# Scan of a Mamba-2 block: the sums of squares over a row's channels, as eight fp32 products on TensorE in place of a VectorE sum and one product

## What is computed

```python
xBC = silu(causal_depthwise_conv(...)); xb, Bc, Cc = split(xBC)      # before the scan
Y_diag = einsum('bcqhn,bcshn,bhcqs,bcshp->bcqhp', Cm, Bm, Lm, xdt)    # within a chunk of 128 rows
states = einsum('bcqhn,bhcq,bcqhp->bchpn', Bm, decay_states, xdt)     # carried from chunk to chunk
Y_off  = einsum('bcqhn,cbhpn,bhcq->bcqhp', Cm, prevs, exp(dAc))
y = (Y_diag + Y_off).reshape(b, l, h, p) + Dp * x_h
y = y.reshape(b, l, 1024)
y = y * silu(z)
y = y * rsqrt(mean(y * y, axis=-1) + eps) * norm_w                    # the sums of squares of the change
h = residual + y @ out_proj_w                                         # then a second norm, h2
```

## Time and profile before

| what | value |
|---|---|
| median of 3 runs | 1661.74 us (1661.3 to 1663.65) |
| the profiled execution | 1666.47 us |
| its span, first to last instruction | 1664.8 us |
| mean granted TensorE clock | 0.942 |
| TensorE busy | 1445.6 us (87%) |
| VectorE busy | 780.0 us (47%) |
| ScalarE busy | 446.8 us (27%) |
| GpSimd busy | 441.1 us (26%) |
| the scan | about 338 to 646 us |
| one chunk of the scan, in its steady part | 17.50 us |

### The profile page before, as it was taken

The page is one execution under the profiler, slowest core; times in us unless marked ns, Lnnn a source line. Parts: engine busy times, 40 slices in busy tenths (PEclk is TensorE's granted clock), DMA queues, the critical chain, the costliest instruction groups (busy, mean ns, idle before and its releaser), DMA issues. The chain is left out here.

```text
span 1664.8 us, 20088 instructions
## 1 busy us (share of the span) xinstructions
PE 1445.6 (87%) x6651; PEld 1045.3 (63%) x6652; DVE 780.0 (47%) x1357; ACT 446.8 (27%) x924; POOL 441.1 (26%) x486
## 2 busy tenths in 40 slices
PE   5688979769999994999999999999760599999996
PEld 4566768536666663888888888888620355555553
DVE  4857676658998992323232323233544122122121
ACT  4333434345555552212112121121120111111110
POOL 2411111126776764101011111010006222222222
PEclk9899999979999997999999999999985799999998
DMA  8112202352332314801000010000197222223220
GB/s 179 51 51 102 101 28 100 127 171 89 107 116 96 121 58 170 289 17 32 20 25 25 16 34 17 22 0 0 53 364 262 87 78 86 87 82 86 89 77 21
DMA packets 92867, 147.12 MB, mean 88 GB/s; under 512 B 29182, under 2 KB 45566, under 8 KB 92800
## 3 DMA queue, kind: packets, MB, share of 16 engines
q1 hardware_dynamic: 79424, 119.92, 22.0%
q0 software_dynamic: 8800, 25.21, 4.5%
q10 hardware_dynamic: 4576, 1.13, 0.3%
HBM read 91.63 MB, written 58.27 MB: 90 GB/s over the span
## 5 line engine op out<-in xcount | busy, mean ns | idle before, releaser
L1356 PE MATMUL ff_bank<-ff_hT_hi,ff_w_hi 128*128 128x512 f32 x512 | 202.3, 395 | 13.3 <-POOL ff_w_lo L1262 13.3
L1356 PE MATMUL ff_bank<-ff_hT_hi,ff_w_lo 128*128 128x512 f32 x512 | 204.9, 400 | 0.0
L1356 PE MATMUL ff_bank<-ff_hT_lo,ff_w_hi 128*128 128x512 f32 x512 | 203.0, 396 | 0.0
L1797 PE MATMUL ex_bank<-w_gu,xT 128*128 x624 | 193.5, 464 | 1.4 <-ACT xT L1728 0.8
L1322 DVE TENSOR_TENSOR ff_prod<-ff_prod,ff_bank 128x512 f32<-128x512 f32 x64 | 44.0, 688 | 274.7 <-PE ff_bank L1356 266.3
L1262 POOL TENSOR_TENSOR ff_w_lo<-ff_stage,ff_w_hi 128x1024 fp32r<-128x1024 f32 x24 | 57.3, 2393 | 417.2 <-ACT ff_w_hi L1309 413.6
L1797 PEld LDWEIGHTS ex_bank<-w_gu,xT 128*128 128x128 f32 x624 | 116.7, 192 | 60.9 <-issue 3.8
L1767 DVE SCALAR_TENSOR_TENSOR result_rows<-ex_bank,xs,result_rows 128x512 f32<-128x512 f32 x39 | 29.3, 751 | 256.2 <-DMA result_rows<-out_dram,xs 253.6
L479 DVE SCALAR_TENSOR_TENSOR conv_acc<-raw,conv_w,conv_acc 128x512 f32<-128x512 f32 x144 | 114.9, 799 | 62.4 <-ACT raw L296 52.5
L572 PE MATMUL pj_bank<-hT_hi,w_in_hi 128*128 128x512 f32 x336 | 140.3, 418 | 1.6 <-DVE hT_lo L412 1.6
L572 PE MATMUL pj_bank<-hT_lo,w_in_hi 128*128 128x512 f32 x336 | 137.5, 409 | 0.0
(11 more groups left out here) (238 smaller groups left out, 2429.9 us busy)
## 6 DMA issues: line engine op xcount, KB each, us to landing
cv_rows<-cst SPq DMA_DIRECT2D x12, 1024.0 KB, 4.3
cv<-cv_rows SPq DMA_DIRECT2D x16, 768.0 KB, 4.3
sorted_rows<-blank SPq DMA_DIRECT2D x1, 10023.0 KB, 46.0
xs<-sorted_rows SPq DMA_DIRECT2D x39, 257.0 KB, 2.7
zs_rows<-zst SPq DMA_DIRECT2D x8, 1024.0 KB, 6.5
zs<-zs_rows SPq DMA_DIRECT2D x16, 512.0 KB, 5.3
w_gu<-in_L_ffn_Wg_dram SPq DMA_DIRECT2D x8, 704.0 KB, 10.7
w_gu<-in_L_ffn_Wu_dram SPq DMA_DIRECT2D x8, 704.0 KB, 11.5
```

The costliest lines, as they stand in the source:

```text
L1356: mm = eng.matmul(ps, w[a], x[b], start=first and i == 0, stop=last and i == 2)
L1797: mm = eng.matmul(ps[:, 0:EI], xT[v % 2][:, k, :], w_gu[:, i, bass.ds(e * KD + k, 1), :].rearrange("p a n -> p (a n)"), start=(k == 0), st ...
```

## The change

The reduction on VectorE, its buffer `sqs` and its semaphore go. TensorE's `row_sums` waits for the squares of both halves and makes eight fp32 products, one for each block of `sq`, that add up in the same two columns of `a_ps`. ScalarE, which may not overwrite `sq` before it is read, waits for the products (`rs`) of the chunk before instead of for the reduction. The place of `row_sums` in TensorE's order and its wait for `ebx` stay.

```diff
         sq = sb("sq", [P, NB, P])
-        sqs = sb("sqs", [P, P])
@@ ScalarE, high(e, a)
                 eng.activation(y_hi[a][:, :, :], yg[a][:, :, :], ACT.Copy).then_inc(s["hi"], 1)
-                ge(eng, s["sqs"], e)
+                ge(eng, s["rs"], e)
                 eng.activation(sq[:, a * HPG:(a + 1) * HPG, :], yg[a][:, :, :], ACT.Square).then_inc(s["sq"], 1)
@@ VectorE
-            def squares(e):
-
-                eng.wait_ge(s["sq"], 2 * e + 2)
-                ge(eng, s["rs"], e)
-                eng.tensor_reduce(sqs[:, :], sq[:, :, :].rearrange("p k q -> p q k"), AX_X, ALU.add).then_inc(s["sqs"], 1)
-
@@ VectorE, the pass
                     new_carry(e)
-                    squares(e)
@@ TensorE, row_sums(e)
-                eng.wait_ge(s["sqs"], e + 1)
+                eng.wait_ge(s["sq"], 2 * e + 2)
                 eng.wait_ge(s["ebx"], min(2 * (e + 1) + 1, 2 * TILES))
-                eng.matmul(a_ps[:, 0:2], sqs[:, :], ones[:, 0:2], start=True, stop=True).then_inc(s["rs"], 1)
+                for n in range(NB):
+                    last = eng.matmul(a_ps[:, 0:2], sq[:, n, :], ones[:, 0:2], start=(n == 0), stop=(n == NB - 1))
+                last.then_inc(s["rs"], 1)
```

More of the change, by code:

```diff
@@ L675, in ssd @@
             "wo_dma", "v_dma", "wo_hi", "wo_lo", "consts",
-            "seg", "exp", "cb", "score", "ebc", "ebx", "cexp", "yd", "yo", "ysum", "gate", "hi", "lo", "sq", "sqs", "rs",
+            "seg", "exp", "cb", "score", "ebc", "ebx", "cexp", "yd", "yo", "ysum", "gate", "hi", "lo", "sq", "rs",
             "rsum", "r", "out", "h", "hsq", "h2_step", "h2T", "h2_hi", "h2_lo", "turn", "xb_row", "xdt", "xdd",
```

## The result

The changed kernel takes 1682.4 us as the median of 4 runs (1681.1 to 1683.7), the kernel before, on the same chip, 1662.7 us. The ratio is 1.0117, with a 95% interval of 1.0099 to 1.0134: slower by 1.2%, as forecast (1681.1 us, range 1677 to 1700). The sum, 19.4 us, agrees with the 19.7 us between the medians, but partly by luck: the scan itself grew by 17.9 us in the profiled executions, and two terms of the sum were off in opposite directions.

A forecast was written before the change was run, and what follows sets the result against it. The prediction took TensorE to set the scan's pace: 14 chunks at 1.43 us (20.0), plus 1.1 for the first, minus 0.1 and 1.6 for the last, gave +19.4 on 1661.7, so 1681.1 us, range 1677 to 1700.

The forecast's parts named there:

- TensorE sets the pace, the delay carries through: In the scan, TensorE bounds each chunk, so the added products delay all behind them, 1.43 us a chunk.
- 0.1125 us a pair, by the distance of loads: Each added load-and-MATMUL pair costs the distance between loads, 0.1125 us; 14 pairs make 1.575 us a chunk.
- The wait at 0.14 us a chunk: Ahead of the small product, TensorE's wait for VectorE's reduction costs 0.14 us in a regular chunk, which the change removes.
- 0.39 from load to load: Time from the small product's load to turn_h2's, taken as 0.39 us as before, plus 1.575 for the added pairs.
- First chunk 1.1 us more: In the scan's first chunk, added products cost 1.575 us and 0.49 us of wait goes: 1.08 us more.
- Last chunk: At the scan's end, TensorE's wait for VectorE goes: 0.1 us won, 1.6 more if small products hold the clock.
- Waits costed at nothing: Changed waits of TensorE and ScalarE, and VectorE's copy ahead of cum_rows, were to add no time in a chunk.
- The first rival: Narrow products let the clock fall in about half of 15 chunks, 10 to 18 us on top; 35%, 1690 to 1700.
- The sum's case: The sum as it stands over the scan, clock held, pairs at 0.10 to 0.12 us: 50%, 1677 to 1684 us.
- cheaper pairs: Rival for the added pairs in the scan: 0.07 us each, 10.6 us more in all, 1672 us; 5%.
- without overlap: Rival for the scan's added pairs: loads paid in full, 0.188 us a pair, 37 us more, 1699 us; 5%.
- the 25 ns of the rival: Added pairs in the scan nearly free at 25 ns each, 0.4 us more, 1662 us; as good as no change, 2%.

The follow-up runs named there:

- split: Changed kernel with four of the eight products left in place and four moved behind the second b_dot_c; 1682.3 us, ratio 1.0114.
- wide: Changed kernel with its eight products given 128 moving columns of ones in place of two; 1678.6 us in a single run.
- the two kernels with sixteen of them: Changed kernel with each of the eight products made twice: with two moving columns 1726.6 us, with 128 columns 1711.0 us, single runs.
- the one-product kernel: Changed kernel with one product over one block of squares in place of eight, VectorE's reduction still out; 1654.6 us in a single run.
- the kernel with VectorE's dead sum: Changed kernel with VectorE's reduction put back, read by nobody, ScalarE waiting for it too; 1682.4 us, ratio 1.0108.

## Right and wrong, step by step

- **TensorE sets the pace, the delay carries through.** Right: 1.57 us more on TensorE from one product to eight are 1.57 us more a chunk, and VectorE's work can be there or not.
- **0.1125 us a pair, by the distance of loads.** Right: 0.111 to 0.112 in the kernels with eight and sixteen products, narrow or wide. Neither bound was near, neither 0.07 nor 0.188.
- **The wait at 0.14 us a chunk.** Wrong: 0.30. The step that failed is the one that took "0.39 from load to load" as what stands behind the product in any case. The chunk became longer by 1.27 and not 1.43 us, and where the sum has 20.0 it is 14 x 1.27 = 17.8 us.
- **First chunk 1.1 us more.** The wait went as told (0.17 in front of the loads in place of 0.66). Its distance to the next has a fall of the clock in it: 19.84 us, where 18.3 to 18.4 stood with none (18.27 split, 18.38 wide). That is 1.5 us more than the sum has. That the products brought this one fall is likely from the two kernels with sixteen of them, and not shown by itself: ahead of the first sums the clock fell in every kernel, at places that differ from trace to trace.
- **Last chunk.** Right in kind, and larger than told. The first load comes together with the last out_proj product of the half (648.91), not 0.31 us behind it, and turn_h2 1.82 us behind that load, where 0.39 + 1.575 were taken: the 0.39 had the wait in it again. So turn_h2 gained 0.60 us (2.42 to 1.82 behind that product) and not 0.1. From that product to the feed-forward it was 27.99 us (630.45 to 658.44) and is 25.84 (648.91 to 674.75): 2.15 won, 1.7 forecast. The clock stays up behind the sums, but the condition given for it, that the small products hold the clock, isn't what did it: in the one-product kernel, with two pairs only and no idle time ahead of them, it stayed at 1.00 too (622.6 to 629.4). What had gone was the idle time.
- **Waits costed at nothing.** Right: VectorE's copy is at 469.05 in the shown chunk, cum_rows comes 2 us behind, and the gaps ahead of TensorE's other groups of loads are as long as before.
- **The first rival.** The mechanism was right and its share wrong. Narrow products don't hold the clock, a fall costs 1.5 us, but in the profiled execution of the changed kernel it came in one chunk of 15 and not in half of them. The 1.8 us of products there lie between products that stream; twice as many, 3.6 us, brought it in half the chunks. One of 15 is no rate, though: from the second chunk on the products always lay in the same two places against the changes of the granted clock, and the kernel with VectorE's dead sum, with the same order on TensorE, had two falls. The sum's case and the rival's are thus one case with few falls, and the 35% and the 50% weren't exclusive.
- **Sums of the rivals.** With cheaper pairs turn_h2 of the last chunk comes earlier as well, which the sums left out or took too low: they make 9.9 us at 0.07 and -0.2 at 0.025 a pair, where 10.6 and 0.4 stand, and 36.3 without overlap, where 37 stands. None was near the measured time.
- **Made up for each other, in part.** The scan in three parts, beside the prediction's terms:

| part of the scan | forecast | measured |
|---|---|---|
| its start to the second chunk's sums | +0.9 us | +2.2 us, 1.5 of it the fall |
| 13 distances | +18.6 | +16.5 |
| the last distance and all behind it | -0.1 | -0.8 |
| together | +19.4 | +17.9 |

The wait taken too low made the forecast too high by 2.1 us in the middle, and the fall that the sum didn't have gave 1.5 back. The other 1.8 us up to the 19.7 between the medians aren't in the scan. A sum that comes within 0.3 us of the medians isn't right in its terms for it.

The Trainium skill, "TensorE: Matmul & The Clock Gate", section "LDWEIGHTS (loading the stationary operand)", gives columns / 1.2 ns for a load, which makes 107 ns for 128 columns, and these traces agree (111 ns from load to load, in one pass or two). In its section "Back-to-back issue gap" the 25 ns of the rival are those of a product alone; for a stream of loads and products the same section says that both set the spacing, and gives about 81 ns a product at 128 columns. Here, where every pass has a load of its own, it was 111 to 112 ns with 2 columns and with 128, and the measurement decides.

## What to carry to other kernels

Where a sum over many blocks goes to TensorE as products with a few columns, it is paid by the load: count loads, not columns, and ask which engine sets the pace before taking work from one that doesn't. Try first whether a short wait goes away when the waiting product changes places with its neighbour in the engine's order: that cost nothing here and gave 7 us, where the work moved to the bound engine cost 20. Read the price of a wait on both sides of the waiting instruction, against the same place in a kernel where nothing is waited for.

## Not expected of the hardware

- 128 moving columns cost as good as nothing over two beside a 128x128 fp32 load: 18.82 and 18.77 us a chunk with 16 pairs in it, 20.61 and 20.56 with 32.
- A stretch in which TensorE's MATMULs and loads were both busy for 3.40 of 3.40 us, with two moving columns each, was followed by a granted clock of 0.53; with 128 columns and the same loads by 1.00. Busy shares didn't tell here whether the clock would hold.
- A 128x128 load has the same distance of 0.111 us for a one-pass product as for each pass of an fp32 one.
- A product that waited for another engine also set back the group behind it, by 0.16 us net. Why it does was not tried.
